# Row-tiled mixing, folds in twos inside the projections, and other loads of the feed-forward weights

## The reference, cut to what matters

```python
agg_w = einsum('bk,koi->boi', att, weight)         # a 32x32 mixing matrix per sequence, from the condition
y = einsum('boi,bih->boh', agg_w, x) + agg_b       # mixes the 32 rows of each sequence
x = x + attention(y)                               # 32 heads, 8 key groups, causal over 32 rows, then Wo, bo
c = conv1d(x, 32 channels in 4 groups, 9 taps) + ctx + bias
h1, h3 = c @ (w1 + 2*B1 A1).T, c @ (w3 + 2*B3 A3).T   # LoRA of rank 16; 512 -> 1376
x = x + (silu(h1) * h3) @ (w2 + 2*B2 A2).T
```

## Time and profile before

| what | us |
|---|---|
| median of 3 runs | 604.81 |
| lowest, highest | 600.99, 606.08 |
| the profiled execution's own time | 603.86 |
| its span, first to last instruction | 602.1 |
| granted TensorE clock, mean over the span | 0.987 of full |

### The profile page before, as it was taken

How to read it: one execution, slowest core, us unless ns; L and a number is a source line. 1 busy time by engine, 2 the same in 40 slices (tenths; PEclk the granted TensorE clock), 3 DMA queues, 4 the chain that set the end, 5 groups by cost and what they waited for, 6 DMA issues and landing times.

```text
span 602.1 us, 7725 instructions
## 1 busy us (share of the span) xinstructions
PE 579.9 (96%) x3035; PEld 463.6 (77%) x3035; DVE 240.8 (40%) x340; ACT 172.7 (29%) x296; POOL 182.0 (30%) x131
## 2 busy tenths in 40 slices
PE   9996999979998979999999999999999999999997
PEld 6994888757776658888778888768888767888885
DVE  1431544589999853111453111325111144111112
ACT  3561212556654343333221111113111112111110
POOL 3445491778999865544400000000000000000000
PEclk9997999989999989999999999999999999999999
DMA  6997747645467677000008300004600001200001
GB/s 239 276 208 219 241 149 262 174 134 137 122 178 176 190 253 165 0 1 0 1 0 224 73 0 1 1 1 140 155 0 0 0 0 70 70 1 0 1 1 70
DMA packets 70798, 59.22 MB, mean 98 GB/s; under 512 B 45136, under 2 KB 61904, under 8 KB 69648
## 3 DMA queue, kind: packets, MB, share of 16 engines
q1 hardware_dynamic: 69904, 57.43, 34.2%
q10 hardware_dynamic: 864, 1.38, 0.6%
HBM read 40.94 MB, written 16.79 MB: 96 GB/s over the span
## 4 chain that ended last, share of the span: by engine, by line
PE 75%; DMA 13%; SPq 6%; POOL 2%; DVE 2%; issue 1%; ACT 1%; ACTq 0%; DVEq 0%; POOLq 0%
PE twin L1317 41%; PE twin L1338 20%; DMA f_sb<-in_f 6%; PE twin L1143 5%; DMA x_dram<-rows 4%; SPq L467 2%; DMA rows<-x_dram 2%; PE twin L1215 2%; PE twin L1283 2%; SPq L497 2%; PE twin L1163 1%; PE twin L1176 1%; PE twin L1132 1%; POOL wo_lo L626 1%; SPq L446 1%
## 5 line engine op out<-in xcount | busy, mean ns | idle before, releaser
L1034 DVE TENSOR_TENSOR gate<-twin,gate 128x512 f32<-128x512 f32 (+1 forms) x44 | 30.4, 691 | 246.2 <-PE twin L1317 246.2
L1317 PE MATMUL twin<-c_hi,f_lo 128*128 128x512 f32 (+1 forms) x352 | 96.7, 397 | 4.2 <-POOL f_lo L671 4.2
L1317 PE MATMUL twin<-c_hi,f_hi 128*128 128x512 f32 (+1 forms) x352 | 96.3, 396 | 0.0
L1317 PE MATMUL twin<-c_lo,f_hi 128*128 128x512 f32 (+1 forms) x352 | 95.6, 394 | 0.0
L1317 PEld LDWEIGHTS twin<-c_hi,f_lo 128*128 128x128 f32 (+1 forms) x352 | 65.6, 187 | 20.4 <-POOL f_lo L671 4.6
L1317 PEld LDWEIGHTS twin<-c_hi,f_hi 128*128 128x128 f32 (+1 forms) x352 | 66.0, 188 | 15.9 <-issue 0.3
L1317 PEld LDWEIGHTS twin<-c_lo,f_hi 128*128 128x128 f32 (+1 forms) x352 | 65.9, 187 | 15.7
L857 ACT ACTIVATE gate<-twin 128x512 f32<-128x512 f32 (+1 forms) x44 | 26.3, 598 | 171.5 <-PE twin L1317 171.5
L1338 PE MATMUL twin<-f_lo,gate_hi 128*128 128x512 f32 (+1 forms) x176 | 68.5, 389 | 0.0
L860 ACT CAST gate_hi<-gate 128x512 fp32r<-128x512 f32 (+1 forms) x44 | 27.3, 620 | 128.7 <-DVE gate L1034 128.7
L1338 PE MATMUL twin<-f_hi_head,gate_hi 128*128 128x512 f32 x128 | 50.2, 392 | 0.0
(11 more groups left out here) (150 smaller groups left out, 818.1 us busy)
## 6 DMA issues: line engine op xcount, KB each, us to landing
f_sb<-in_f SPq DMA_DIRECT2D x8, 688.0 KB, 24.5
x_dram<-resid_stage SPq DMA_DIRECT2D x16, 256.0 KB, 2.2
rows<-x_dram SPq DMA_DIRECT2D x16, 256.0 KB, 3.4
q_t<-q_dram SPq DMA_DIRECT2D x8, 512.0 KB, 4.2
x_dram<-rows SPq DMA_DIRECT2D x16, 256.0 KB, 3.4
rows<-x_dram SPq DMA_DIRECT2D x8, 512.0 KB, 4.4
out<-rows SPq DMA_DIRECT2D x12, 256.0 KB, 2.0
f_sb<-in_f SPq DMA_DIRECT2D x1, 2560.0 KB, 11.5
```

What stands on the lines that cost most here:

```text
L1034: dve.tensor_tensor(gate[0:w, h % 2, :], up_bank[2 * (h % 2) + 1][0:w, :], gate[0:w, h % 2, :], ALU.mult).then_inc(gate_ready, 1)
L1317: mm = pe.matmul(bank[0:w, :], f[:, c, :], c_part[:, c, :], start=(n == 0 and c == 0), stop=(n == 2 and c == DC - 1))
```

## The change

- Mixing: each 128-row matmul becomes four of 32 rows, one per sequence, with 32 moving columns, each sequence b of a tile into a bank of its own (`mix_bank` = ps[2:6]): 64 matmuls a block. DVE waits until all four column quarters are mixed, and adds in two instructions of 256 columns per quarter, each over two banks. Two waits of PE move or come new ahead of blocks 0 and 1.
- Folds: two in the middle and two at the end of a projection, from K on, with two banks.
- f3 and f1: one transfer each, with another order of the rows over the partitions; the factors and the convolution's input are read in the same new order (a stride of two in its moving operand).
- f2: three row ranges and the rest, at n = 7, 15 and 18 of SP's loop.
- The first convolution: groups 0 and 1 a step earlier than 2 and 3.

```diff
@@ names and banks
-USES = DC + 1 + REP + 1
+USES = 2 + REP
-        a_part = up_part[2 * S:3 * S, 0:2 * D].rearrange("k (x r l) -> k x r l", r=2, l=S)
-        a_up = up_sb[:, 0:2 * D].rearrange("k (x l r) -> k x r l", r=2, l=S)
+        a_part = up_part[2 * S:3 * S, 0:2 * D].rearrange("k (y x l) -> k y x l", x=BT, l=S)
+        a_up = up_sb[:, 0:2 * D].rearrange("k (y l x) -> k y x l", x=BT, l=S)
-        fold_bank = ps[4:8]
+        fold_bank = ps[6:8]
+        mix_bank = ps[2:6]
-        f2_loads = [(f2_sb[:, 0:HC - 1, :], f2[0:(HC - 1) * P, :].rearrange("(c p) d -> p c d", p=P)),
-                    (f2_sb[0:HW[-1], HC - 1, :], f2[(HC - 1) * P:HID, :])]
+        f2_loads = [(f2_sb[:, a:b, :], f2[a * P:b * P, :].rearrange("(c p) d -> p c d", p=P))
+                    for a, b in ((0, 4), (4, 8), (8, HC - 1))]
+        f2_loads += [(f2_sb[0:HW[-1], HC - 1, :], f2[(HC - 1) * P:HID, :])]
@@ SP
             for f_sb, f in ((f3_sb, f3), (f1_sb, f1)):
-                for part in range(4):
-
-                    sp.dma_start(f_sb[part * S:(part + 1) * S, :, :],
-                                 f.rearrange("(h l r) c j -> h r l c j", h=2, r=2)[part // 2, part % 2])\
-                        .then_inc(ffn_loaded, 16)
+                sp.dma_start(f_sb[:, :, :].rearrange("p c j -> p (c j)"),
+                             f.rearrange("(l x) c j -> x l (c j)", x=BT)).then_inc(ffn_loaded, 16)
...
-                if n == QUADS + 1:
+                if n == 7:
+                    load_f2(0)
+                if n == QUADS - 1:
 
                     for half in range(2):
                         sp.wait_ge(k_loaded[half], 16 * G * BLOCKS)
+                    load_f2(1)
+                if n == QUADS + 2:
+
                     sp.wait_ge(v_spread, 2 * BT * BLOCKS)
-                    for dst, src in f2_loads:
-                        sp.dma_start(dst, src).then_inc(f2_loaded, 16)
+                    load_f2(2)
+                    load_f2(3)
@@ DVE
-                        dve.wait_ge(front_filled, blk * USES + c + 1)
-                        dve.tensor_tensor(y_t[:, c, :], front[c % 2][:, :],
-                                          mixb_all[:, blk * BLOCK:(blk + 1) * BLOCK], ALU.add)\
-                            .then_inc(front_emptied[c % 2], 1)
+                        dve.wait_ge(mixed, (blk + 1) * DC)
+                        for pair in range(2):
+                            own = slice(2 * pair, 2 * pair + 2)
+                            to, shift = (a.rearrange("p (t b s) -> p b t s", b=BT, s=S)[:, own] for a in
+                                         (y_t[:, c, :], mixb_all[:, blk * BLOCK:(blk + 1) * BLOCK]))
+                            banks = twin[1 + pair][:, :, c * P:(c + 1) * P].rearrange("p b (t s) -> p b t s", s=S)
+                            add = dve.tensor_tensor(to, banks, shift, ALU.add)
+                        add.then_inc(y_shifted, 1)
@@ PE
             def project(blk, j, folds):
...
                         mm = pe.matmul(front[n % 2][:, :], w[:, c, :], y[:, c, :],
                                        start=(m == 0 and c == 0), stop=(m == 2 and c == DC - 1))
-                mm.then_inc(front_filled, 1)
+                        if (m, c) in ((1, 1), (2, DC - 1)) and folds:
+                            if m == 2:
+                                mm.then_inc(front_filled, 1)
+                            for _ in range(2):
+                                fold_up(folds.pop(0))
+                            mm = None
+                if mm is not None:
+                    mm.then_inc(front_filled, 1)
...
+                    if blk == 0:
+
+                        pe.wait_ge(mix_shift_spread[0], 16)
+                        pe.wait_ge(shifts_act, 1)
+                    if blk == 1:
 
                         pe.wait_ge(mix_made, 2)
                         pe.wait_ge(mix_made_act, 4)
                     for c in range(DC):
-                        bank_free(c)
                         for t in range(TILES):
-                            mm = pe.matmul(front[c % 2][:, t * P:(t + 1) * P], buf[:, t, c * P:(c + 1) * P],
-                                           mix[:, blk * TILES + t, :, :].rearrange("p c o -> p (c o)"),
-                                           start=True, stop=True)
-                        mm.then_inc(front_filled, 1)
+                            for b in range(BT):
+                                own = slice(b * S, (b + 1) * S)
+                                mm = pe.matmul(mix_bank[b][:, c * P + t * S:c * P + (t + 1) * S],
+                                               buf[own, t, c * P:(c + 1) * P], mix[own, blk * TILES + t, b, :],
+                                               start=True, stop=True)
+                        mm.then_inc(mixed, 1)
...
-                        if c % 2:
-                            bank_free(c + 2)
+                        pe.wait_ge(y_shifted, blk * DC + c + 1)
...
                     mm = pe.matmul(bank[part, :], conv_sb[:, g, :, :, :].rearrange("k h r o -> k (h r o)"),
-                                   near[g][:, :, half * S:(half + 1) * S], start=True, stop=True)
+                                   near[g].rearrange("k b (l h) -> k h b l", h=2)[:, half], start=True, stop=True)
...
-                if n == QUADS:
-
-                    pe.wait_ge(conv_packed, 1)
-                    pe.wait_ge(scores_turned, QUADS)
-                    for g in range(GROUPS):
+                if n in (QUADS - 1, QUADS):
+
+                    pe.wait_ge(scores_turned, n)
+                    for g in range(2):
+                        g += 2 * (n - QUADS + 1)
                         convolve(0, g, first_conv_bank[g])
```

More of the change, by code:

```diff
@@ L122, in adaln_attention_ffn @@
         causal_loaded = sem("causal_loaded")
+        mixed = sem("mixed")
+        y_shifted = sem("y_shifted")
         front_filled = sem("front_filled")
@@ L448, in store_queries @@
             def store_queries(i):
-                for n in (DC + REP, DC + REP + 1):
+                for n in (REP, REP + 1):
                     sp.wait_ge(front_emptied[n % 2], i * (USES // 2) + emptied(n) + 1)
@@ L475, in _ @@
                     sp.dma_start(wo_sb[:, :, :], wo).then_inc(wo_loaded, 16)
-                    sp.wait_ge(front_filled, i * USES + DC)
+                    sp.wait_ge(mixed, (i + 1) * DC)
                     for tile in range(TILES):
                         load_resid(tile)
-                    sp.wait_ge(front_emptied[1], i * (USES // 2) + emptied(DC + 1) + 1)
+                    sp.wait_ge(front_emptied[1], i * (USES // 2) + emptied(1) + 1)
                     sp.wait_ge(q_stored[0], 16 * BLOCKS // 2)
@@ L499, in load_near, with load_f2 @@
                         .then_inc(near_loaded[g // 2], 16)
+            def load_f2(part):
+                dst, src = f2_loads[part]
+                sp.dma_start(dst, src).then_inc(f2_loaded, 16)
             def load_conv_shift(i):
@@ L619, in _ @@
                         .then_inc(resid_ready, 1)
-            pool.wait_ge(front_filled, (BLOCKS - 1) * USES + DC + 1)
+            pool.wait_ge(front_filled, (BLOCKS - 1) * USES + 1)
             pool.memset(v_wide[:, :, :, :, :], 0.0).then_inc(v_cleared, 1)
@@ L717, in copy_queries @@
             def copy_queries(blk, j):
-                n = DC + 2 + j
+                n = 2 + j
                 act.wait_ge(front_filled, blk * USES + n + 1)
@@ L727, in _ @@
                     for c in range(DC):
-                        act.wait_ge(front_emptied[c % 2], blk * (USES // 2) + emptied(c) + 1)
+                        act.wait_ge(y_shifted, blk * DC + c + 1)
                         act.copy(y_hi[:, c, :], y_t[:, c, :]).then_inc(y_hi_ready, 1)
@@ L734, in _ @@
                             act.copy(wkq_hi[:, 1 + c, :, :], wq_sb[:, :, c, :]).then_inc(wkq_hi_split, 1)
-                    n = DC
+                    n = 0
                     act.wait_ge(front_filled, blk * USES + n + 1)
@@ L739, in _ @@
                         .then_inc(front_emptied[n % 2], 1)
-                    n = DC + 1
+                    n = 1
                     act.wait_ge(front_filled, blk * USES + n + 1)
@@ L786, in round_conv @@
                              c_raw[:, g, :, :, :]).then_inc(c_hi_ready, 1)
-            act.wait_ge(front_emptied[DC % 2], emptied((BLOCKS - 1) * USES + DC) + 1)
+            act.wait_ge(front_emptied[0], emptied((BLOCKS - 1) * USES) + 1)
             act.wait_ge(v_cleared, 1)
@@ L934, in _ @@
                         dve.wait_ge(up_fold_filled, n + 1)
-                        dve.scalar_tensor_tensor(out=dst, in0=fold_bank[n % 4][:, 0:FOLD_N], scalar=LORA_SCALE,
+                        dve.scalar_tensor_tensor(out=dst, in0=fold_bank[n % 2][:, 0:FOLD_N], scalar=LORA_SCALE,
                                                  in1=dst, op0=ALU.mult, op1=ALU.add).then_inc(up_folded, 1)
@@ L1000, in _ @@
```

(26 more changed lines are left out.)

9 lines of the change are left out of this document (4 added, 5 removed).

## The result

The changed kernel takes 665.45 us (median of 4 runs, 657.33 to 669.70), the kernel before 604.99 us beside it: ratio 1.097, 95% interval 1.085 to 1.108. It is slower by 60 us; the prediction said 675, range 618 to 690. The slowest of the four runs (669.70 us) is left out of the ratio, since it is more than 1.5% above the fastest. The profiled execution is the fastest: 657.33 us with a span of 655.5, so the trace has to account for 53.4 us more span than before.

The account below looks back on a forecast made before the run. The prediction took the kernel as bound by TensorE, busy 96% of the span, with two waits on its chain. 603.9 + 76.3 + 1.4 + 0.8 - 7.3 = 675 us; range 618 to 690 us.

Parts of the forecast that it names:

- The up weights: Load before PE's first fold: four engines carry it, PE restarts at 130 us instead of 53.72, +76.3 us.
- between 13.0 and 25.4 I take nearly the low one: Up-weight load: GB/s per engine taken near 13.0, as engines walking 32 partitions apart share ports; 108 us in full step.
- rival B: Up-weight load: four engines out of each other's way, 25.4 GB/s each, data at 82 us, total 627 us; chance 0.27.
- 53.6 less 5.64/0.215: Up-weight load: the sum by which the first f data were put at about 26 us.
- rival C: Up-weight load: all 16 engines at full rate, first wait and its slow clock gone, total 590 us; chance 0.17.
- Folds in twos: First fold moves into the middle of block 1's K projection; six matmuls now come after the wait, +1.4 us.
- Mixing: Blocks 2 and 3, mixing to K: DVE adds only after all mixing, +0.4 us a block, +0.8 in all.
- I take 2.4 us, nearer the floor: PE's 64 small mixing matmuls a block: 2.4 us, between a floor of 1.7 and a ceiling of 6.9.
- K starts at 2.4 + 5.45: Blocks 2 and 3: K starts 7.85 us after mixing begins, behind DVE's adds, y_lo and handing over; 7.44 before.
- Blocks 0 and 1 mix before the wait: Mixing of the first two blocks precedes PE's wait for the up weights, so only blocks 2 and 3 count.
- End of the attention: PE's wait for f_lo: f2 in pieces and convolutions 0 and 1 moved forward, -7.3 us, bounds -8 and -3.
- Stride two in the convolutions: Feed-forward blocks: the moving operand read with stride two costs 0, bounded by 11 us.

Follow-up runs that it names:

- plain loads: Changed kernel with both up weights' rows laid out in partition order ahead of the launch, one 128-partition load per matrix: 606.74 us, ratio 1.0036.
- the run with two engines: Changed kernel with each up weight in two loads of 64 partitions, the source's outermost dimension 2: 713.68 us in one run.
- the kernel before with plain loads: Kernel before, its own row order laid out ahead of the launch, one 128-partition load for each up weight: 595.63 us, ratio 0.9865.
- the filled wait: Changed kernel with plain loads, plus four fp32 matmuls put into PE's wait between mixing and V: 603.69 us, ratio 0.9993.
- without their split: Kernel before with plain loads and the down weight in three pieces, first convolutions where they were: 590.79 us, ratio 0.9777.

## Why the prediction was right, and where its sizes were off

**The up weights, +76.3 forecast, +52.6 measured.** The mechanism is shown: the outermost dimension of 4 deals the load to four engines, plain loads take the hole away, and outermost dimension 2 makes it deeper. This is what the Trainium skill says (DMA: Bandwidth & Descriptors, Why a DMA increments its semaphore by 16 and not by 1), and the traces agree with it for 2, 4, 32 and 128. The mis-sized step is "between 13.0 and 25.4 I take nearly the low one": the engines were taken to walk in step to the end. Over the whole load, 24.4 to 105.6 us by the packet records, they moved 5.64/81.2/4, or 17.4 GB/s each, with packets of 1.63 us at its start and 0.82 at its end. So they stay in each other's way for a part of the load only, and rival B's argument, that a lead of a few rows lasts once it is there, was right for the rest. The prediction's last packets were put at 130 us and came at 106. Rival B (82 us) had the other end; the truth lies between, 24 us from either. Nothing in the prediction chose that middle: its range held because it reached from B to the forecast. What sets how soon the engines part isn't settled, and it may be why this kernel's four runs spread by 12 us. One sum is off besides: 53.6 less 5.64/0.215 is 27.4 us and not 26, while the first packet record before is at 24.6.

The half rate of the kernel before was read rightly from the earlier trace rows: plain loads over 128 partitions run at 435 GB/s. The Trainium skill's SBUF — State Buffer, Door 1, has 32 partitions reach half of the ports that 128 reach; the traces agree, 217 against 431 to 435 GB/s. The time of rival C, 590 us, is to be had, but by a layout and with the old mixing.

**Folds in twos, +1.4 forecast, +2.3 measured.** The six matmuls are there; most of the missing 0.9 us is that the granted clock stays at 0.50 for 5.4 us from the first fold on instead of 3.9. The length of the wait alone doesn't set this: after the 107.70 us of the run with two engines it was 4.7. The folds in pairs cost nothing, as forecast: in the version with plain loads K to the next mixing is 67.78 - 51.29 = 16.5 us, in the kernel before with plain loads 61.14 - 44.84 = 16.3.

**Mixing, +0.8 forecast, +5.1 measured.** Two steps failed. "I take 2.4 us, nearer the floor": it is 3.77 us, in the middle of the bounds 1.7 and 6.9, since the records come 28 ns apart and not 13.4. And "K starts at 2.4 + 5.45": with 3.77 it would be 9.2 us by that chain; the filled wait shows that chain, 9.12 us where the clock held. The measured 10.01 comes by another, mixing 3.77, wait 1.04, V 5.2 at the falling clock, and DVE's y_lo is no longer the last. The fall of the clock, 0.9 us a block, stood in no term of mine. "Blocks 0 and 1 mix before the wait" was right, and hid 6.4 us: with the wait gone, the four blocks cost 12.9.

**End of the attention, -7.3 forecast, -7.2 measured.** The pieces of f2 do it (6.0 alone). That the convolutions have to move forward for it is not borne out: 590.79 us without their split and 591.47 with it.

**Stride two in the convolutions, 0:** right, the rest of the span differs by 0.4 us.

Together the forecast for the profiled execution was 71.2 us more, and it was 53.4: -23.7 from the load, +0.9 from the folds, +4.3 from the mixing, +0.7 in small parts. The median hides some of this, because the profiled execution was the fastest.

## What to carry to other kernels

Look at the outermost dimension of both sides of every large DMA before its bytes: a reorder of rows written as a small outer step takes engines away, and one that stays inside 32 partitions takes half the rate; the same reorder made in the layout ahead of the launch costs nothing on the chip, and was worth 1.3% to the kernel before as it stood. Splitting each mixing matmul into four of a quarter of the rows gained 0.2 us of 3.96 in a mixing, and made a block 2.6 us longer and more, by DVE's later start and the fallen clock. And when a change sits in front of a long wait, price it as if the wait were gone, since whoever mends the wait will pay it.

## What the runs showed of the hardware that was not expected

- Matmuls on four row groups of 32, weights of 128 columns and 32 columns moving: one record every 28 ns in turn, 60 ns on one group at a time, both at a granted clock of 1.00; the block-diagonal form on 128 rows has one every 124 ns.
- A run of them with PE busy throughout brought the granted clock from 1.00 to 0.50; a pause of 0.88 us behind matmuls on 128 rows left it at 1.00.
- Four engines that write partitions 32 apart took 0.82 to 1.73 us for 22 KB, 1.11 in the median, and became faster as the load went on; sixteen inside 32 partitions took 1.72 in the median, sixteen over 128 partitions 0.82.
